# Regrouped query/key rows, scores of two heads in row tiles, and a ring of eight heads of probabilities

## What is computed

```python
xn = _layernorm(x)
qkv = einsum('bsm,qhdm->bqhsd', xn, W_qkv)               # 16 heads of 64 dimensions
qk_rot = qk * cos + _rotate_half(qk) * sin               # the first 32 dimensions of q and k alone
scores = where(causal, -inf, einsum('bhqd,bhkd->bhqk', Q, K)) / sqrt(64)
out = einsum('bhqk,bhkd->bhqd', softmax(scores), V)      # then W_o
ffn = sum over the 2 best of 9 choices of gate * (gelu(x w1) w2)   # 8 experts; the ninth is x itself
```

## Time and profile before

| | |
|---|---|
| Median of three runs | 1653.41 us (1646.27 to 1653.52) |
| Profiled execution, first to last instruction | 1643.9 us |
| Median of the runs over that span | 9.5 us |
| PE busy | 1341.7 us (82%) |
| ACT busy | 1174.3 us (71%) |
| DVE busy | 1143.8 us (70%) |
| POOL busy | 987.4 us (60%) |
| Mean granted TensorE clock | 0.943 of 2.4 GHz |

### The profile page before, as it was taken

The page is one execution under the profiler, slowest core; times in us unless marked ns, Lnnn a source line. Parts: engine busy times, 40 slices in busy tenths (PEclk is TensorE's granted clock), DMA queues, the critical chain, the costliest instruction groups (busy, mean ns, idle before and its releaser), DMA issues.

```text
span 1643.9 us, 48543 instructions
## 1 busy us (share of the span) xinstructions
PE 1341.7 (82%) x13156; PEld 1038.9 (63%) x13157; DVE 1143.8 (70%) x4325; ACT 1174.3 (71%) x3758; POOL 987.4 (60%) x1697
## 2 busy tenths in 40 slices
PE   2529999999999999999999999999977999576620
PEld 1417766777666776766777667766656988455520
DVE  6788776777777777767777777777756777354531
ACT  7409887888888888878888878888877888334310
POOL 3208777777777787777777777776760000454555
PEclk9859999999999999999999999999998999788865
DMA  9623544334553335543345433355423333222242
GB/s 302 164 49 83 115 115 102 86 84 97 115 119 87 86 84 109 120 104 86 85 93 117 117 91 85 84 110 117 105 89 94 87 85 85 72 77 77 79 129 64
DMA packets 125894, 166.49 MB, mean 101 GB/s; under 512 B 15504, under 2 KB 85392, under 8 KB 125456
## 3 DMA queue, kind: packets, MB, share of 16 engines
q1 hardware_dynamic: 117296, 147.50, 37.6%
q0 software_dynamic: 8416, 17.33, 3.6%
HBM read 30.42 MB, written 33.69 MB: 39 GB/s over the span
## 4 chain that ended last, share of the span: by engine, by line
POOL 30%; issue 20%; PE 18%; DMA 16%; DVE 7%; another core or an unknown queue 3%; ACT 2%; DVEq 1%; POOLq 1%; SPq 1%; ACTq 0%
DMA sorted_x_dram<-send_x,send_at 15%; POOL probs L433 8%; POOL probs L432 7%; POOL arena L417 7%; PE bank L1034 4%; PE bank L1033 4%; PE bank L1035 4%; POOL arena L422 4%; POOL sorted_x_dram L437 3%; PE bank L1132 1%; PE bank L1166 1%; PE bank L1118 1%; DVE arena L690 1%; POOL arena L482 1%
## 5 line engine op out<-in xcount | busy, mean ns | idle before, releaser
L577 ACT ACTIVATE probs<-arena,neg_max 128x128 f32<-128x128 f32 (+1 forms) x1024 | 455.4, 448 | 126.5 <-DVE neg_max L887 112.1
L432 POOL TENSOR_TENSOR probs<-probs,inv_total 128x128 f32<-128x128 f32 x512 | 208.2, 407 | 247.8 <-DMA sorted_x_dram<-send_x,send_at 126.4
L1118 PE MATMUL bank<-ident,probs 128*128 128x128 f32 x1536 | 263.2, 280 | 70.6 <-POOL probs L433 62.6
L887 DVE CUSTOM_DVE_ANT_0 arena<-bank,causal 128x128 f32<-128x128 f32 (+1 forms) x1024 | 314.9, 345 | 0.0
L482 POOL DMA_INDIRECT arena<-sorted_y_dram,slots x128 | 123.7, 967 | 273.6 <-DMA sorted_y_dram<-arena 171.6
L1118 PEld LDWEIGHTS bank<-ident,probs 128*128 128x128 f32 x1536 | 173.6, 141 | 144.9 <-issue 87.9
L894 DVE RECIPROCAL inv_total<-total 128x2 f32<-128x2 f32 x512 | 82.9, 162 | 254.4 <-PE bank L1109 178.1
L433 POOL TENSOR_SCALAR probs<-probs,inv_total 128x256 f32<-128x256 f32 x512 | 251.4, 491 | 0.0
L417 POOL TENSOR_TENSOR arena<-arena 128x256 f32<-128x256 f32 x256 | 189.8, 752 | 64.0 <-DVE arena L849 58.8
L1033 PE MATMUL bank<-xnT_lo,wqk_hi 128*128 (+1 forms) x768 | 212.2, 276 | 10.7 <-DVE arena L855 10.2
L1035 PE MATMUL bank<-xnT_hi,wqk_hi 128*128 (+1 forms) x768 | 212.1, 276 | 0.0
(11 more groups left out here) (158 smaller groups left out, 3675.6 us busy)
## 6 DMA issues: line engine op xcount, KB each, us to landing
second<-arena SPq DMA_DIRECT2D x128, 256.0 KB, 4.2
arena<-arena SPq DMA_DIRECT2D x128, 256.0 KB, 4.1
second<-arena SPq DMA_DIRECT2D x128, 128.0 KB
arena<-arena SPq DMA_DIRECT2D x128, 128.0 KB
arena<-sorted_x_dram SPq DMA_DIRECT2D x80, 128.0 KB
sorted_y_dram<-arena SPq DMA_DIRECT2D x80, 128.0 KB
sorted_x_dram<-arena SPq DMA_DIRECT2D x3, 2560.0 KB, 21.2
arena<-experts_dram SPq DMA_DIRECT2D x8, 512.0 KB, 4.5
```

The lines of the kernel that those rows point to most:

```text
L432: nc.gpsimd.tensor_tensor(p0, p0, inv_total[:, s % 4, 0:1].broadcast_to([P, P]), ALU.mult)
L577: last = nc.scalar.activation(probs[:, s % 4, at:at + w], masked[:, s % 2, at:at + w], ACT.Exp, bias=neg_max[:, s % 2, t:t + 1], scale=-1. ...
L887: last = nc.vector.tensor_tensor_reduce(out=masked[:, s % 2, at:at + w], in0=SC[s % 2][:, at:at + w], in1=causal[:, at:at + w], scale=1.0, ...
L1118: last = nc.tensor.transpose(TP[s % 2][:, k * P:(k + 1) * P], probs[:, s % 4, k * P:(k + 1) * P], ident[:])
```

## The change

Five things change together.

1. The q/k weights are laid out anew. A unit now has 16 rows for each of 8 (rotated and unrotated) pieces: two heads of each of four groups. The swapped partner rows go: `rope` needs 4 units, not 8. `turn` makes two products for a unit (with cos and with sin, both from the same bank) and `rope_add` is one subtraction and one addition of 256 columns. `by_cos` and `by_sin` exist once, where `turned` had two buffers; `turn` waits for the `rope_add` before it.
2. Stacking takes 4 transfers for q and 4 for k, each from 32 partitions to 128, in pieces of 2 KB. `q_stack` and `k_stack` now hold one head in partitions 0 to 63 and another in 64 to 127.
3. `scores` runs every second slot, for two heads: per query half three products (lo·hi, hi·lo, hi·hi) of 64 rows, each for both heads in turn, one head in each bank. Since both banks are written together, it waits until both heads before have been masked.
4. `probs` and the sums hold 8 heads. The lags become 4, 5, 7, 8 (from 3, 4, 5, 6).
5. Psum banks: two for the units (from three), two for the product with V (from one). Units move in `BESIDE`: one per slot.

```diff
+PROLOGUE = [("rest", 0), ("rest", 1), ("rope", 0), ("rope", 1), ("rest", 2), ("rest", 3), ("rope", 2), ("rope", 3),
+            ("v_low", 0), ("v_low", 1)]
 BESIDE = [
-    [("rest", 0)], [("rest", 1), ("rope", 0)], [("rope", 1)], [("rope", 2), ("rope", 3)],
+    [("rest", 0)], [("rope", 0)], [("rest", 1)], [("rope", 1)],
...
-PJ_BANKS = 3
-INV_LAG, T_LAG, OUT_LAG, PV_LAG, O_LAG = 2, 3, 4, 5, 6
+PJ_BANKS = 2
+LO_HI = ((1, 0), (0, 1), (0, 0))
+INV_LAG, T_LAG, OUT_LAG, PV_LAG, O_LAG = 2, 4, 5, 7, 8
+HELD = 8
...
-        PJ, SC, TP = bank[0:3], bank[3:5], bank[5:7]
-        PV = bank[7][:, 0:SEQ]
+        PJ, SC, TP = bank[0:2], bank[2:4], bank[4:6]
+        PV = [b[:, 0:SEQ] for b in bank[6:8]]
...
+            def stack(of, to, done, r):
+                sp.dma_start(to[:, r, :, :, :].rearrange("p l u n -> p (l u n)"),
+                             of[32 * r:32 * r + 32, :, :, :, :].rearrange("p c l u n -> p c (l u n)")).then_inc(done[r], 16)
             def stack_q(n, parity):
-                sp.wait_ge(q_rope_lo, 4 * n + 4)
+                sp.wait_ge(rest_lo, 4 * n + 2)
+                sp.wait_ge(q_rope_lo, 2 * n + 2)
                 for r in range(GRP):
-                    for half_at in range(2):
-                        sp.dma_start(q_stack[parity][64 * half_at:64 * half_at + 64, r, :, :].rearrange("p l n -> p (l n)"),
-                                     q_staged[32 * r:32 * r + 32, :, :, :].rearrange("p k l n -> p (k l n)")).then_inc(q_stacked[r], 16)
+                    stack(q_part, q_stack[parity], q_stacked, r)
...
-                nc.gpsimd.tensor_tensor(roped[j % 4], t[:, 0:SEQ], t[:, SEQ:2 * SEQ], ALU.add).then_inc(rope_sum, 1)
+                nc.gpsimd.tensor_tensor(r[:, 0, :], by_cos[:, 0, :], by_sin[:, 1, :], ALU.subtract)
+                nc.gpsimd.tensor_tensor(r[:, 1, :], by_cos[:, 1, :], by_sin[:, 0, :], ALU.add).then_inc(rope_sum, 1)
...
-                    raw(wqk_hi[:].rearrange("p g n -> p (g n)"), raw_qk)
+                    for at, of in WQK:
+                        last = nc.scalar.activation(by_head(wqk_hi[:, at, :]), of, ACT.Copy, scale=W_SCALE)
...
-                if not (isinstance(m, int) and m == 0 and j < 2):
-                    dve.wait_ge(rope_sum, 8 * m + j - 1)
-                nc.vector.tensor_tensor(turned[j % 2], psum[:], rot_q if j < NG else rot_k,
-                                        ALU.mult).then_inc(turn_done, 1)
+                if not (isinstance(m, int) and m == 0 and j == 0):
+                    dve.wait_ge(rope_sum, ROPES * m + j)
+                nc.vector.tensor_tensor(by_cos, both(psum), cos, ALU.mult)
+                nc.vector.tensor_tensor(by_sin, both(psum), sin, ALU.mult).then_inc(turn_done, 1)
...
                 if not (first and s < 2):
-                    pe.wait_ge(s_masked, G - 1)
-                for at, w in ((0, P), (P, 2 * P)):
-                    qs = slice(0, P) if at == 0 else slice(P, 2 * P)
-                    dst = SC[s % 2][:, at:at + w]
-                    q_lo, q_hi = (q_stack[parity][:, s // NG, l, s % NG * SEQ + qs.start:s % NG * SEQ + qs.stop] for l in (1, 0))
-                    mm(dst, q_lo, k_stack[parity][:, s, 0:w], start=True, stop=False)
-                    last = mm(dst, q_hi, k_stack[parity][:, s, 0:w], start=False, stop=True)
+                    pe.wait_ge(s_masked, 16 * b + s)
+                for qs, at, w in ((slice(0, P), 0, P), (slice(P, SEQ), P, SEQ)):
+                    for n, (ql, kl) in enumerate(LO_HI):
+                        for h in range(2):
+                            rows = slice(64 * h, 64 * h + 64)
+                            last = mm(SC[h][:, at:at + w], q_stack[parity][rows, r, ql, u, qs], k_stack[parity][rows, r, kl, u, 0:w],
+                                      start=(n == 0), stop=(n == 2))
...
-                if not (first and j < 1):
-                    pe.wait_ge(o_done, 8 * b + j)
+                if not (first and j < 2):
+                    pe.wait_ge(o_done, 8 * b + j - 1)
...
+                    if s % 2 == 0:
+                        scores(b, s, parity, first)
```

More of the change, by code:

```diff
@@ L236, in attention_and_experts, with head_rows, by_head @@
         out_tiles = out.rearrange("b (t p) d -> p (b t) d", p=P)
+        def head_rows(unit, c):
+            g = 8 * (unit // 2) + 4 * (c // 2) + 2 * (unit % 2)
+            dims = slice(c % 2 * 16, c % 2 * 16 + 16)
+            return raw_qk[:, g:g + 2, :].rearrange("p g (r n) -> p r g n", r=GRP)[:, :, :, dims]
+        WQK = [(4 * unit + c, head_rows(unit, c)) for unit in range(4) for c in range(4)]
+        def by_head(w):
+            return w.rearrange("p (r g n) -> p r g n", r=GRP, g=2)
         def evicted(b, s):
@@ L255, in beside, with parts, both @@
                     for n, (at, kind, j) in enumerate(units_of(first, last)) if at == s]
-        def parts(which, rest, g, n=1):
-            at = slice(g * SEQ, (g + n) * SEQ)
-            if which == 0:
-                return q_staged[:, rest, 0, at], q_staged[:, rest, 1, at]
-            return k_staged[:, 0, rest, at], k_staged[:, 1, rest, at]
+        def parts(kind, j):
+            of, first_c = q_part if j < 2 else k_part, 0 if kind == "rope" else 2
+            return [of[:, first_c:first_c + 2, l, j % 2, :] for l in range(2)]
+        def both(psum):
+            return psum[:].rearrange("p (c t) -> p c t", c=2)
         def owner(kind, b):
@@ L451, in sample @@
                     for kind, j, u, psum, n in beside(b, first, last, s - 3):
-                        if kind == "rope" and j < NG:
+                        if kind == "rope" and j < 2:
                             q_rope_low(j, b + 1)
@@ L1141, in sample @@
                     if not (first and s < T_LAG):
-                        transposes(G - T_LAG, (s - T_LAG) % 4, None if first and s < T_LAG + 2 else
+                        transposes(G - T_LAG, (s - T_LAG) % HELD, None if first and s < T_LAG + 2 else
                                    evicted(b, s - T_LAG - 2) if s >= T_LAG + 2 else evicted(b - 1, s - T_LAG - 2 + H))
```

170 lines of the change are left out of this document (87 added, 83 removed).

## The result

The changed kernel takes 1609.28 us (median of four runs, 1608.54 to 1612.73) against 1653.47 us (1646.27 to 1656.93) for the kernel before on the same chip: ratio 0.9746, 95% interval 0.972 to 0.9773. It is 44 us faster, not the 94 us of the forecast. The sign was right, the size was half, and 1609 lies inside the wide range and outside the forecast's own (1525 to 1600).

What follows compares the result with a forecast made beforehand. GpSimd with its waits was taken as the period, 35.1 us a sample; -2.5 - 0.1 + 0.4 - 1.0 = -3.2, times 31 samples = -99, +5 outside, gave 1560 us (own range 1525 to 1600, wide 1490 to 1640).

Steps and rivals of the forecast that it cites:

- GpSimd with its waits is the period: Attention: GpSimd's 26.5 us busy plus 8.6 idle make the 35.1 us of a sample.
- Rival D: Attention: sends wait as long as before at other slots, no change in time, about 1655 us; chance 5%.
- The stacking term: Smaller q transfers let the send of slot 9 land sooner, shortening GpSimd's wait before slot 12: gain 2.5 us per sample.
- The cover: TensorE (28.6 us) and ScalarE (28.5) get shorter but lie beneath GpSimd's 31.9, so they add nothing to the sum.
- The longer pipeline: GpSimd may fall one slot further behind before transposes wait; with a shorter front, 1.0 us less inverse waits per sample.
- TensorE's steps: Scores of a pair take 0.49 us side by side, each switch of tile shape 0.09; TensorE 28.6 us per sample.
- Rival B: Scores on TensorE: the row tiles do not run side by side, 1630 us; chance 15%.
- The handover of single-buffered scores: Between VectorE's masks and TensorE's next pair: 1.06 us each, 8.5 per sample, covered by about 8 us of VectorE work.
- rival C: Slower: the handover of the single-buffered score banks becomes the bound, 1714 us; chance 10%.
- Low parts, additions and roundings: GpSimd's two q low parts take 2.6 us, eight additions stay at 0.752 each; ScalarE's four roundings take 0.630 each.
- the +0.4: GpSimd's additions wait for two VectorE products of the turn, not one: 0.4 us more per sample.
- Outside the loop: Weight splitting +1.8 us, prologue +2, pipeline end +1: together +5 us.

Runs made afterwards that it cites:

- Run 4: Kernel before the change with its second send in slot 5, not slot 9: 1637.68 us, ratio 0.9912.
- run 1: Changed kernel with V held in two buffers, by parity of the sample: 1577.32 us, ratio 0.9545.
- Run 3: Changed kernel with scores of one head per slot in the same 64-row form, each bank freed by itself: 1736.83 us, ratio 1.0461.
- run 2: Changed kernel with the old lags (3, 4, 5, 6), the ring of eight heads kept: 1591.88 us, ratio 0.9622.
- run 6: Changed kernel with V held twice, three score banks and one bank for the product with V: ratio 0.9458 to the kernel before on its chip.
- run 5: Changed kernel with V held twice and the matmul units of a sample's second half spread: ratio 0.9449 to the kernel before on its chip.
- run 7: Changed kernel with V held twice, rows for the experts made ready in slot 1 and first send in slot 2: ratio 0.9806.
- run 9: Changed kernel with V held twice and units moved (V high to slots 6 and 7, last rotated k part to slot 9): 1667.72 us, ratio 1.0094.

## Why the prediction was right or wrong

**GpSimd with its waits is the period: wrong, and the step that failed first.** The prediction added 26.5 busy and 8.6 idle and took each wait removed for time won. Busy plus idle of any engine is the period, whoever sets the pace, so the sum of 35.1 us showed nothing about GpSimd. Run 4 took 73 us of send waits away and got 69 back as another wait, for a net gain of 0.52 us per sample in place of 2.5, and of 1.7 at most. The changed kernel lost 96 us of send waits, 3.2 us per sample, and its period fell by 1.53. And run 1, which changes nothing on GpSimd, gained 1.14. Rival D (5%) comes nearest, with a wait that returns at another place; but it had the sends wait as long as before, and no change in time.

**The stacking term, 2.5 us of the 3.2: its mechanism right, its size not.** The send of slot 9 lands in 4.41 us on average, from 5.68 (forecast 3.3 from 5.9), all sends at 2.5 at the median, from 3.1:

```profile
DMA to landing us min/median/max: 2.3/2.5/7.1
```

It now meets the k transfers, issued from 21.0 us of the sample on, 0.6 us behind it; before it met those of q. The wait for sends fell even further than forecast (30.1 us, not 55): in front of the `scale` of slot 12 GpSimd now waits 1.2 us per sample for VectorE's inverse sum and 0.3 for the send, where it waited 2.8 us for the send before. The forecast put 2.5 us on the term; run 4 makes it 0.5 to 1.7 in the kernel before.

**The cover: costed at nothing, and worth something.** TensorE's shorter work (29.5 us busy in a period against 32.4) and ScalarE's (27.5 against 29.1) stood in the sum at zero, because they lay beside GpSimd. Run 3 speaks against that for TensorE: 4.8 us more of it made the period 3.9 us longer, though at a TensorE load above that of both kernels. Run 1's period is 2.67 us below before's. Between 0.5 and 1.7 of it can be the sends (run 4) and 0.5 the lags (run 2 against run 1); the rest, 0.5 to 1.7 us, is left to the regrouped rows and paired scores. That split assumes that the parts add up, which no run shows.

**The longer pipeline: a wait overlooked.** "GpSimd may fall one slot further behind" was counted at -1.0; it gives -0.52 where V has two buffers. What the prediction did not follow is who waits for `pv_done`: moving the product two slots on brought it into the slot of the copy that overwrites V. It stood in the sum at nothing. Its price is 1.14 us per sample, 35 us by periods and 32 between the medians of run 1 and the changed kernel, most of the 49 us by which the change fell short of the forecast.

**TensorE's steps: right.** After, in slots of the same kind as in the earlier trace rows:

```profile
640.00 0.67 PE L1130 MATMUL bank<-arena 64*128 64x128 f16 x12 [0.76 <-DVE neg_max L912]
640.61 0.39 PE L1059 MATMUL bank<-wvo_lo,xnT_hi 128*128 128x512 f16 x1
```

The twelve matmuls of a pair and the switch behind them take 0.61 us; the forecast was 0.49 + 0.09. The two heads' matmuls start 3 to 4 ns apart, and the last of the twelve starts 0.40 us after the first. A step across a change of shape is 0.20 us, 0.11 within one shape: 0.09 again. Rival B (1630) falls with the 0.61 us. About 4 ns between the starts of two row groups is what the Trainium skill has in TensorE: Matmul & The Clock Gate (Part 3, The mechanism), and the trace agrees. The Trainium skill's drain at a change of tiling mode (TensorEngine Tiling, Key Properties) agrees too, at 0.09 us here.

**The handover of single-buffered scores: right.** VectorE waits 45.7 us for L1130, 1.5 per sample, where rival C asked for 9, and the third bank of run 6 gives 0.43 us per sample. TensorE does wait for masks, as the 0.76 us above shows, and VectorE is busy then.

**Low parts, additions and roundings.** In place of the earlier trace rows:

```profile
L432 POOL TENSOR_TENSOR arena<-arena 128x256 f32<-128x256 f32 x121 | 99.9, 826 | 35.3 <-DVE arena L877 35.3
L433 POOL TENSOR_TENSOR arena<-arena 128x256 f32<-128x256 f32 x121 | 87.7, 725 | 0.0
L553 ACT ACTIVATE arena<-arena 128x512 f16<-128x512 f32 x122 | 76.9, 631 | 53.0 <-POOL arena L433 53.0
L438 POOL TENSOR_TENSOR arena<-arena 128x512 f16<-128x512 f32 x60 | 69.7, 1162 | 0.0
```

Two low parts take 2.3 us (forecast 2.6), an addition 0.826 and 0.725 us (0.75), a rounding 0.631 (0.630). The wait for the turn did not grow (35.3 us from 37.9), so the +0.4 did not come. GpSimd is busy for 78% of the window, not 83%, since the period is longer than forecast.

**Outside the loop: +12.6 us for +5.** The weights split in 32 pieces of 0.223 us, not 0.159:

```profile
L688 DVE SCALAR_TENSOR_TENSOR wqk_lo<-arena,wqk_hi 128x64 f16<-128x64 f32 x32 | 4.4, 223 | 0.0
```

They overlap in part and take 4.4 us for 3.3, +1.1 (forecast +1.8). From the first matmul of the prologue to the router's first instruction on VectorE are 20.4 us, from 16.4, +4.0 (forecast +2). The first mask comes 6.5 us later. The time from the last mask to the end is 6 us more (forecast +1): the first matmul of an expert starts 4.0 us later after it (TensorE idle for 10.9 us in front, not 7.7), and the rest takes 2.1 us more.

**Sum.** From first to last mask -45.4 us, outside +12.6: -32.9 between the two executions. Forecast were -99 and +5. Of the forecast's -3.2 per sample -1.53 came, because -2.67 was there to have and 1.14 was lost to the copy of V. That -2.67 comes so close to -3.2 is in part luck: a gain sized 1.5 to 5 times too large on GpSimd stood for one on TensorE and ScalarE costed at nothing.

What now sets 31.7 us is not settled. In the changed kernel VectorE is almost without a gap in slots 2 to 9 (0.4 and 0.6 us in two of them), GpSimd has no idle time in slots 4 to 7, TensorE none in slots 10 to 14, and at the turn of the sample each waits for another. Runs 5 and 6 bear out that each pair of slots costs what its busiest engine needs there, but the losses of runs 7 and 9 weren't foreseen by it. The two buffers with more units spread or a third bank (ratios 0.9449 and 0.9458) are the best versions found, ahead of the changed kernel's 0.9746. Both edits together, without run 7's, weren't tried.

## What to carry to other kernels

When a lag or a ring changes, list every wait on the semaphores of the moved instruction, the ones of buffers that it frees above all, and put the slot of each beside the new slot of what it waits for: here one copy, two slots of lag and 35 us. Where engines hand work around in a ring, don't take busy plus idle of one for the period; count by pairs of slots what each engine has in them, and expect a wait that is removed to return under another name. A short instruction put in front of work that its engine does without idle time can cost all of its length: a send of 1.1 us made slot 8 longer by 1.2 us in run 4. A transfer that others wait for should be placed by what else is in the DMA engines at its issue, and tried one slot either way: 88 us hung on that.

## What was not expected of the hardware

- The stacking transfers' 2 KB packets took 148 ns on average in attention after the change, with all of them of that size, and 125 ns before, when half were of 4 KB at 318 ns. Two small ones (296 ns) took about as long as one large. The medians are 84 ns for 2 KB in both kernels and 231 for 4 KB.
- An indirect send of 128 rows lands 2.4 us after its issue when the DMA engines are free of stacking transfers (slot 1 of the changed kernel, slot 5 of run 4). Where it meets them, it took 3.3 us (run 9, slot 9) to 5.7 us (before, slot 9) on average.
- In run 9 the granted clock of TensorE fell to 1.2 GHz for a few us in 16 of 30 samples, where TensorE waits 1.8 and 0.8 us on average at the turn of the sample; in the changed kernel, whose longest wait there is 1.2 us on average, it never fell between the first masks of samples 1 and 31.
- Of two additions of one shape on GpSimd the first, L432, takes 0.826 us and the second, L433, 0.725 (means of 121 each). What makes the 0.1 us was not tried.
- One chip ran the experts' stage of the same code in less time: from last mask to end 358 us (run 5) against 428 in the changed kernel elsewhere. In windows of that stage the granted clock is 0.96 there and 0.88 here:

```profile
1210.00:1540.00 330.00, 270.08 (x3006) 231.76 (x3005) 195.76 (x395) 193.38 (x394) 85.70 (x88) 0.88 0.29 78
```

```profile
1160.00:1420.00 260.00, 238.16 (x2886) 213.47 (x2885) 187.41 (x375) 193.36 (x384) 70.96 (x73) 0.96 0.34 94
```

  The clock is 9% higher there and the stage 16% shorter, so the clock isn't all of it; the rest is open.
